# Moving the steps of a seven-product block multiplication one row block, and the rotary products ahead of the outputs, in a fused attention kernel

## What is computed

```
xn  = layernorm(x)
q   = xn @ wq                      # 16 heads of 128 + 64 rotary columns
ckv, k_pe = split(xn @ wkv_a)      # 128 + 64
ckv = rmsnorm(ckv) * kv_norm_scale
k_nope, v = split(ckv @ wkv_b)     # per head 128 + 128
scores = concat(q_nope, rope(q_pe)) . concat(k_nope, rope(k_pe)) * scale, causal
att = softmax(scores) @ v @ wo
mix = sum over 8 factors (xn @ factor) / sqrt(8) + bias
out = x + att + mix
```

## Time and profile before

| | |
|---|---|
| median of 3 runs | 1644.47 us (1640.11 to 1651.82) |
| profiled execution | 1645.56 us, of which the span is 1643.7 us |
| mean granted TensorE clock | 0.975 |
| busy | PE 92%, PEld 49%, DVE 64%, ACT 62%, POOL 63% |
| stage after stage | four pieces to about 590 us, three to 1040, two to 1385, one to the end |

### The profile page before, as it was taken

The page is one execution under the profiler, slowest core; times in us unless marked ns, Lnnn a source line. Parts: engine busy times, 40 slices in busy tenths (PEclk is TensorE's granted clock), DMA queues, the critical chain, the costliest instruction groups (busy, mean ns, idle before and its releaser), DMA issues.

```text
span 1643.7 us, 27314 instructions
## 1 busy us (share of the span) xinstructions
PE 1504.3 (92%) x8340; PEld 803.9 (49%) x8340; DVE 1052.0 (64%) x2627; ACT 1015.9 (62%) x2584; POOL 1038.0 (63%) x1081
## 2 busy tenths in 40 slices
PE   6899999999999989989898989888988888888887
PEld 5544555455555445444444544444444444445453
DVE  7778777777777656555555555555555555566666
ACT  7886777787775765555566656555455555444444
POOL 3788788775775975645677655565477655544453
PEclk9999999999999999999999999999999999999999
DMA  6599999987876886766666666656666656543444
GB/s 214 138 218 204 188 183 189 191 172 148 168 158 142 161 159 135 154 143 138 133 130 134 133 134 147 129 137 133 150 128 125 126 125 131 122 112 92 109 113 105
DMA packets 652256, 240.53 MB, mean 146 GB/s; under 512 B 599888, under 2 KB 614736, under 8 KB 651728
## 3 DMA queue, kind: packets, MB, share of 16 engines
q1 hardware_dynamic: 652112, 238.79, 67.7%
HBM read 75.10 MB, written 20.97 MB: 58 GB/s over the span
## 4 chain that ended last, share of the span: by engine, by line
PE 80%; issue 7%; DVE 6%; ACT 4%; POOL 1%; DMA 1%; SPq 0%; DVEq 0%; POOLq 0%; ACTq 0%
PE ps L557 16%; PE ps L559 15%; PE ps L558 15%; PE ps L753 7%; PE ps L754 6%; PE ps L755 6%; PE ps L758 6%; PE ps L759 6%; ACT ex L1043 2%; DVE gm L1454 1%; POOL st L1783 1%; DVE rden L1486 1%; DVE acc L1507 1%; DVE ps L1456 0%; ACT st L1053 0%
## 5 line engine op out<-in xcount | busy, mean ns | idle before, releaser
L1783 POOL TENSOR_TENSOR st<-ex,st 128x512 f16<-128x512 f32 (+3 forms) x640 | 638.9, 1017 | 514.6 <-ACT st L1053 506.9
L1043 ACT ACTIVATE ex<-ps,nm,scales 128x512 f32<-128x512 f32 (+3 forms) x640 | 452.9, 710 | 530.4 <-DVE nm L1473 529.9
L1454 DVE TENSOR_REDUCE gm<-ps 128x1 f32<-128x512 f32 (+1 forms) x384 | 249.3, 670 | 194.6 <-PE ps L759 191.6
L1053 ACT ACTIVATE st<-ex 128x512 f16<-128x512 f32 (+3 forms) x640 | 343.7, 565 | 6.4 <-ACT ex L1043 0.7
L1507 DVE SCALAR_TENSOR_TENSOR acc<-ps,rden,acc 128x512 f32<-128x512 f32 x256 | 190.2, 747 | 81.5 <-PE ps L559 80.7
L753 PE MATMUL ps<-kTh,q 128*128 128x512 f16 (+3 forms) x640 | 227.6, 356 | 8.1 <-ACT ex L1043 4.7
L754 PE MATMUL ps<-kTl,q 128*128 128x512 f16 (+3 forms) x640 | 227.6, 356 | 0.0
L755 PE MATMUL ps<-kTh,q 128*128 128x512 f16 (+3 forms) x640 | 227.5, 355 | 0.0
L758 PE MATMUL ps<-kRh,q 128*128 128x512 f16 (+3 forms) x640 | 226.7, 354 | 0.0
L759 PE MATMUL ps<-kRl,q 128*128 128x512 f16 (+3 forms) x640 | 225.3, 352 | 0.0
L557 PE MATMUL ps<-pT,vH 128*128 128x512 f16 (+3 forms) x640 | 222.8, 348 | 1.4 <-DMA pT<-st 1.4
(11 more groups left out here) (313 smaller groups left out, 2506.3 us busy)
## 6 DMA issues: line engine op xcount, KB each, us to landing
wS<-w_abs SPq DMA_DIRECT2D x48, 256.0 KB, 3.0
wV<-w_vo SPq DMA_DIRECT2D x48, 256.0 KB, 2.9
pT<-st SPq DMA_TRANSPOSE x640, 3.2
wS<-w_abs SPq DMA_DIRECT2D x24, 384.0 KB, 3.4
fland<-factors_in SPq DMA_DIRECT2D x28, 256.0 KB, 3.1
wP<-w_pe SPq DMA_DIRECT2D x24, 256.0 KB, 2.9
wsq<-wq_in SPq DMA_DIRECT2D x16, 256.0 KB, 3.7
wso<-wo_in SPq DMA_DIRECT2D x16, 256.0 KB, 3.0
```

The lines of the kernel that those rows point to most:

```text
L1043: e.activation(ex[:, n % NEX, 0:keys], s_bank(n)[:, 0:keys], ACT.Exp, bias=nm[:, (i * QT + r) % 4:(i * QT + r) % 4 + 1], scale=scales[:, p ...
L1053: e.activation(stage(n, keys)[:, :, 0, :], ex[:, n % NEX, 0:keys].rearrange("p (t n) -> p t n", n=P), ACT.Copy).then_inc(z["a_pH"], 1)
L1454: e.tensor_reduce(m, b, AX_X, ALU.max).then_inc(z["v_max"], 1)
L1783: e.tensor_tensor(s[:, :, 1, :], ex[:, n % NEX, 0:keys].rearrange("p (t n) -> p t n", n=P), s[:, :, 0, :], ALU.subtract).then_inc(z["g_pL" ...
```

## The change

The order of the list changes, and what hangs on it:

- m1, m2 and m6 all lie in r = 0 of the odd unit, in this order and ahead of `out`; m5 in r = 1 and m3 in r = 2, each behind `out`; in r = 3 only c12 is left (ACT and DVE share), ahead of `pv` in the list; m4 in r = 1 of the even unit lies behind `out`.
- `pe` for unit e lies in r = 0 of unit e-2, directly behind m7 and ahead of `out`. Its DVE and POOL share becomes a kind of its own, `rot`, in r = 2 of unit e-2, and the bank of `pe` is held up to it. In the first 16 units and for the first unit of a chunk, `rot` stays directly behind `pe`.
- ACT takes the snapshot of m1 ahead of the exponentials of row block 0. The snapshots of m6 and m5 stay behind `high_parts` or in `early`.
- The `ffn` units are one later (21, 37, 53), so odd ones. Token sums of the first new chunk, one store and one load of weight sums and the load of `wP` are one or two row blocks earlier.

```diff
-FFN_UNITS = (H - 4,) + tuple(k * H + 4 for k in range(1, NC))
+FFN_UNITS = (H - 4,) + tuple(k * H + 5 for k in range(1, NC))
-... "a_m": ("m1", "c11", "m6", "m5", "c12", "c22", "c21"),
+... "a_m": ("m1", "m6", "c11", "m5", "c12", "c22", "c21"),
-    return [(H - 3 + (n + 1) // QT, (n + 1) % QT) if k == 1 else ...
+    return [(H - 3 + n // QT, n % QT) if k == 1 else ...
     if r == 1:
         if H <= i + 1 < NU and i % 2:
-            out += [("c11", (i + 1) // 2), ("m6", (i + 1) // 2)]
+            out.append(("c11", (i + 1) // 2))
         if H <= i < NU and i % 2 == 0:
-            out += [("c22", i // 2), ("m4", i // 2)]
+            out.append(("c22", i // 2))
     if r == 2:
-        if H <= i + 1 < NU and i % 2:
-            out.append(("m5", (i + 1) // 2))
     if r == 0:
         if H <= i + 1 < NU and i % 2:
-            out.append(("m1", (i + 1) // 2))
+            out += [(step, (i + 1) // 2) for step in ("m1", "m2", "m6")]
         if H <= i < NU and i % 2 == 0:
             out.append(("m7", i // 2))
+            if i + 2 < NU and (i + 2) % H:
+                out.append(("pe", i + 2))
...                                       # behind "out":
-    if r == 0 and H <= i + 1 < NU and i % 2:
-        out.append(("m2", (i + 1) // 2))
+    if r and H <= i + 1 < NU and i % 2:
+        out.append(((None, "m5", "m3", "c12")[r], (i + 1) // 2))
+    if r == 1 and H <= i < NU and i % 2 == 0:
+        out.append(("m4", i // 2))
     for e in range(2, NU, 2):
-        if (i, r) == pe_at(e):
-            out.append(("pe", e))
+        if (i, r) == pe_at(e) and (e < H or e % H == 0):
+            out += [("pe", e), ("rot", e)]
+        if e > H and e % H and (i, r) == (e - 2, 2):
+            out.append(("rot", e))
-    if r == 3 and H <= i + 1 < NU and i % 2:
-        out.append(("m3", (i + 1) // 2))
-LEFT = {"m1": "m3", "m7": "m4"}
+LEFT = {"m1": "c12", "m7": "m4", "pe": "rot"}
                                          # ACT:
-                    early = ("q", "wo", "sqv", "m1", "c11", "m6", "c22") + ...
+                    early = ("q", "wo", "sqv", "m6", "c11", "c22") + ...
+                    for kind, n in fills(i, r):
+                        if kind == "m1":
+                            fill(kind, n)
                     for p in range(last + 1):
                         exps(i, r, p)
                                          # SP:
-                        if (i, r) == (sum_slot(m) + 1, 2):
+                        if (i, r) == (sum_slot(m) + 1, 1 if m == G0 - 1 else 2):
                             store_sums(m)
-... ("lS", (-2, 1), (-2, 3)), ...
+... ("lS", (-2, 1), (-2, 2)), ...
-                    if r == 2 and i % 2 and H <= i + 3 < NU:
+                    if r == (2 if (i + 3) % H == 0 or i < H else 0) and i % 2 and H <= i + 3 < NU:
                         load_pe(i + 3)
```

More of the change, by code:

```diff
@@ L57 @@
 TOKENS_HIGH = ((1, 2), (2, 3), (3, 6), (4, 7))
-STEPS = {"p_m": ("m1", "m2", "m6", "m5", "m3", "m7", "m4"), "a_m": ("m1", "c11", "m6", "m5", "c12", "c22", "c21"),
+STEPS = {"p_m": ("m1", "m2", "m6", "m5", "m3", "m7", "m4"), "a_m": ("m1", "m6", "c11", "m5", "c12", "c22", "c21"),
          "v_m": ("c11", "c12", "c22", "c21"), "g_m": ("c11", "c22", "c21")}
@@ L70, in token_slots @@
 def token_slots(k):
-    return [(H - 3 + (n + 1) // QT, (n + 1) % QT) if k == 1 else ((k - 1) * H + 6 + n // 2, n % 2 * 2) for n in range(9)]
+    return [(H - 3 + n // QT, n % QT) if k == 1 else ((k - 1) * H + 6 + n // 2, n % 2 * 2) for n in range(9)]
 def sum_slot(m):
@@ L1163, in _ @@
                             fill(kind, n)
-                    early = ("q", "wo", "sqv", "m1", "c11", "m6", "c22") + (("sq1",) if i == 0 else ())
+                    early = ("q", "wo", "sqv", "m6", "c11", "c22") + (("sq1",) if i == 0 else ())
                     late = ("parts",) if last >= 2 and (r < 2 or i == 0) else ()
+                    for kind, n in fills(i, r):
+                        if kind == "m1":
+                            fill(kind, n)
                     for p in range(last + 1):
@@ L1184, in _ @@
                             continue
-                        if last < 2 or (r >= 2 and i) or kind not in early + late:
+                        if kind != "m1" and (last < 2 or (r >= 2 and i) or kind not in early + late):
                             fill(kind, n)
@@ L1516, in fill @@
                     blocks_sum(kind, n)
-                elif kind == "m3":
+                elif kind == "c12":
                     block_low(n)
-                elif kind == "pe":
+                elif kind == "rot":
                     q_rope(n)
@@ L2063, in _ @@
                     for m in range(G0):
-                        if (i, r) == (sum_slot(m) + 1, 2):
+                        if (i, r) == (sum_slot(m) + 1, 1 if m == G0 - 1 else 2):
                             store_sums(m)
-                    for kind, at, first in (("lA", (-2, 1), (-2, 1)), ("lS", (-2, 1), (-2, 3)), ("lB", (-1, 0), (-1, 0))):
+                    for kind, at, first in (("lA", (-2, 1), (-2, 1)), ("lS", (-2, 1), (-2, 2)), ("lB", (-1, 0), (-1, 0))):
                         for g in range(G0, 2 * NC * G0 // 2):
```

## The result

| | before | after |
|---|---|---|
| median, us | 1643.53 (1640.11 to 1651.82, 4 runs) | 1536.44 (1535.42 to 1537.31, 4 runs) |
| profiled execution, us | 1645.56 | 1537.31 |
| its span, us | 1643.7 | 1535.5 |
| mean granted clock | 0.975 | 0.999 |

The ratio of the times is 0.9341, with an interval from 0.9305 to 0.9377. The profiled executions differ by 108.2 us, where the forecast had 76; the measured time is 8.6 us under the low end of the range (1545). Of the 108 us some 40 are the clock: (1 - 0.975) x 1643.7 = 41 us were lost to it before, (1 - 0.999) x 1535.5 = 1.5 us after.

A forecast was written before the change was run, and what follows sets the result against it. PE bounds the kernel except for holes and slow clock, together 6.1 to 6.5 us a pair. Stage gains 39 + 32 + 16 = 87 us, less 11 us for the clock: 1645.6 - 87 + 11 = 1570 us, range 1545 to 1608.

The forecast's parts named there:

- "Issue": PE standing still without a releaser named in the profile; a sign, to fall from 84.6 to under 20 us.
- The new wait of m6 behind `rot`: On PE in the odd unit, m6 waits for a snapshot delayed by the earlier `rot`: 2.1 us in the two-piece stage.
- Rival (c): The holes ahead of the output have another cause than L1492, so `pe` only moves; 1640 us, chance 0.05.
- Rival (a): Work fills every hole: POOL and DVE run earlier with PE and the m6 wait vanishes; about 1520 us, chance 0.1.
- Rival (d): Slower: exponentials wait for m1 and PE for exponentials, feeding each other; 1665 us, chance 0.03.
- part 1: `pe` ahead of the even unit's first output shrinks its hole to 0.75-0.85, 0.1 and 0.6-0.75 us for three, two, one pieces.
- Clock: Waits of 2.1 to 2.2 us ahead of m6 may bring the slower clock; 11 us charged, bounds nothing or 23 us.
- One piece: In the one-piece stage 3.95 us of waits stay a pair; gain 2.35 us a pair, 16 us over 7 pairs.
- rival (b): Each m6 wait takes the clock down and the odd unit's first scores wait for c21; 1598 us, chance 0.2.
- Units before 16 and the tail: Earlier token sums, store and load in units 13 to 15 cost nothing; the last pair, without `pe`, gains nothing.
- Part 3, three pieces: With `rot` one row block earlier nothing is pushed in the three-piece stage; ACT is ready 0.3 us after PE.
- Two pieces: In the two-piece stage 2.45 us of waits stay a pair; gain 4.0 us a pair, 32 us over 8 pairs.

The follow-up runs named there:

- experiment 4: Changed kernel with DVE's and POOL's `rot` in r = 3 of unit e-2 in place of r = 2, `pe` still ahead of the output; 1519.08 us.
- experiment 1: Changed kernel with ACT's high part of c12 back in r = 3, beside DVE's share; 1559.53 us.
- experiment 2: Changed kernel with `pe`, `rot` and the load of `wP` back in r = 3 of unit e-2, early high part of c12 kept; 1535.15 us.
- experiment 7: Changed kernel with ACT's high part of c12 in r = 3 and the rotary products in their old place; 1589.9 us.
- experiment 5: Changed kernel with ACT's snapshot of m1 back among or behind the exponentials of row block 0; 1611.45 us.
- experiment 6: Changed kernel with `pe` in the same row block (r = 0) but behind the even unit's first output; 1573.85 us.
- experiment 3: Kernel before with only `pe` moved ahead of `out`, `rot` to r = 2, and the `ffn` units and `wP` load that go with it; 1601.34 us.
- experiment 9: Changed kernel with m2 and m6 behind the odd unit's first output, m1 ahead of it with its early snapshot; 1573.32 us.
- the square: Four kernels: high part of c12 in r = 2 with `pe` ahead of the output 1536 us, `pe` in r = 3 1535; c12 in r = 3, 1560 and 1590.

## Why the prediction missed its range

**Right.** The bound and the cause: PE waited for the low half of `oT`, and work put ahead of the blocked output filled the hole. "Issue" fell from 84.6 to 2.5 us (forecast: under 20). `pe` stands directly behind m7 and in front of the output. The new wait of m6 behind `rot` was worked out as 2.1 us in the two-piece stage and is 2.01 and 2.02; `rot` starts at 1187.65, 10.6 us after the even unit's first output product at 1177.03, and 10.4 was forecast; experiment 4 shows that `rot` makes this wait. Rival (c), another cause of the holes, falls with experiments 1, 2 and 7: both things that should close the hole by the chain through L1492 do. Rival (a) was nearer in time (1520, 16 us too low), but by luck: its reason, an m6 wait that vanishes, did not come true; only experiment 4 brings that about, and it gives 1519. Rival (d), exponentials and PE feeding each other, is not in the trace: no m6 wait is over 2.02 us. In experiment 5, where the snapshot stands behind the exponentials, they reach 3.9 us.

**The step that failed** is in part 1, "DVE's chain gets shorter by about 0.45 us, since c12 goes ahead of the `oT` copy on ACT", and the description of the change has it too: both shares of c12 in r = 3. Only DVE's share lies there. ACT's still hangs on the kind `m3`, so it moved a whole row block earlier, and the chain ACT, DVE, PE that made the long hole was cut at its first link. The size of it is in experiments 7 and 2, both without filler: the hole is 3.29, 2.49 and 3.18 us with the high part in r = 3, and 1.22, 1.07 and 0.75 us with it in r = 2. So the earlier high part shortens the hole by a further 2.1, 1.4 and 2.4 us. The 0.45 us themselves were right for the kernel that I had in mind: 3.13 + 0.66 - 3.29 = 0.50 in the three-piece stage, 0.50 in the two-piece stage and nothing in the one-piece stage. The holes of 0.85, 0.1 and 0.75 us that I left a pair do not exist; that is 0.85 x 8 + 0.1 x 8 + 0.75 x 7 = 13 us on paper, and 23 us by experiment 1, where they are 0.70, none and 0.59 and where the stage ends and a clock of 0.996 come in. Between the marks that kernel takes 3.6 us longer than the changed one from 13 to 15 and 9.3, 3.9 and 8.1 us in the three later stages. With c12 where I had it, the kernel takes 1559.5: inside the range, and what the sum gives without the 11 us for the clock (1559). That closeness is partly luck: this kernel gains 6.0, 33.4, 29.8 and 19.0 us between the marks where the sum has 0, 39, 32 and 16.

**Terms that were mis-sized.**
- *Clock*: 11 us charged for m6 waits of 2.1 to 2.2 us; none of these waits (2.01, 2.02) took the clock down here, and it is 0.999. In experiment 6 the same waits did, in 4 of 6 cases, so the charge was not wrong in kind.
- *One piece*: I left 3.95 us of waits a pair. m6 waits 1.25 to 1.32 instead of 2.2 (0.76 and 0.78 in two pairs, behind a wait of 0.4 for a load of `wS`), the second output 0.41 instead of 0.55, m3 some 0.1 instead of 0.45, the hole of part 1 0 instead of 0.75; the first scores of the odd unit wait 0.40 for c21, which I had only in rival (b). The sum is 2.2. A pair takes 23.99 us instead of 24.95, which is 7 us over the stage; by its marks the stage has 11 of the 32 us that the gain was larger than forecast; the other 4 lie at its ends. The failed step is in this: 8.1 us by experiment 1. The clock is another 11.
- *Units before 16 and the tail*: costed at nothing. Between the marks of 13 and 15 a wait of 3.96 us in unit 16 went and 4.5 us were won, of which experiment 1 gives back 3.6; in the last unit PE now waits 3.28 us for POOL's low part (L1750), 0.98 before.
- *Part 3, three pieces*: 0.3 us of m6 wait forecast, none found; 42.8 us came instead of 39. A pair takes 48.91 us instead of 49.75, but the last one has no `pe`, keeps a hole of 1.22 us and gains 4.4 us only.

Two pieces came out near: 33.7 us for 32. In part this is luck: a pair takes 37.64 us instead of 37.25, so it gains 3.6 us and not 4.0; that only six of the eight have the wait of m6, and the ends of the stage, make up for it.

**What stays open.** Why a hole takes the clock down or not. Before, 6 of 7 holes of 2.33 us did; the m6 waits of 2.01 us did in 0 of 6 cases in the changed kernel and in 4 of 6 in experiment 6; 2.49 us did in 1 of 6 and 3.29 in 3 of 6 in experiment 7; 3.17 in all 6 in experiment 3 and in 5 of 6 in experiment 9; in experiment 5, 3.08 in 5 of 8 and 3.92 to 3.93 in all 6. No experiment changed the length alone, so what decides beside it was not separated. It is also open which of the parts that all four corners of the square have in common bring the 50 us.

## What to carry to other kernels

When an in-order engine is blocked on a product, look at both ends: what it could do meanwhile, and which link of the chain in front is queued too late. Here either cure closed a good part of the same hole (55 and 30 us alone), and together they gave nothing more than the better one, or 16 us more once the filler's reader stood well (experiment 4). So do not forecast them as a sum: the second cure has only what the first leaves. Put the filler ahead of the blocked instruction, but its reader behind the work that the next stage needs (experiment 4: 17 us for one number). And when a list of kinds drives several engines, look up each kind in each engine's branch: a step that "moves" may move on one engine only, and that was what the forecast missed here.

## What the runs showed of the hardware

A slow stretch costs more than its hole. Eight us from the start of a 2.33 us hole in the kernel before, and of a 2.02 us wait in the changed one (columns as in Rows 3):

```profile
1281.00:1289.00 8.00, 5.94 (x26) 3.11 (x27) 5.29 (x15) 2.81 (x9) 3.26 (x4) 0.79 0.55 108
```
```profile
1108.00:1116.00 8.00, 6.03 (x34) 3.32 (x35) 3.80 (x8) 4.10 (x13) 3.81 (x4) 1.00 0.62 81
```

PE counts as busy about as long in both (5.94 and 6.03 us), but the first has the mean clock 0.79, part of it at 1.2 GHz and the rest at 2.4: (1 - 0.79) x 8 = 1.7 us of full speed are lost, on top of the hole. The pairs of experiment 6 say the same: with the 2.01 us wait and a slow stretch behind it they take 40.5 us, with the wait alone 38.9.

The Trainium skill (page "TensorE: Matmul & The Clock Gate", section "Why this matters for your kernels") warns of the slower clock only for gaps longer than the 2.33 us ones here. The traces here do not agree: 2.01 and 2.33 us were enough in some places. Nor was a longer one always enough: after 3.29 us the clock stayed up in 3 of 6 cases (experiment 7).
